# Attention stage of a transformer block: column sums on POOL and VectorE, reciprocals through DRAM, output weights split ahead

## The reference, cut to what matters

```python
q = (xn @ Wq).reshape(B, S, 4, 4, 32); k = (xn @ Wk).reshape(B, S, 4, 32); v = ...
scores = einsum('bqkgd,bskd->bkgqs', q, k) * scale      # causal mask
attn = softmax(scores)                                  # float32
out = einsum('bkgqs,bskd->bqkgd', attn, v).reshape(B, S, 512)
x = x + out @ Wo + moe(xn)
```

## Time and profile before

| what | us |
|---|---|
| median of three runs | 3688.0 |
| the profiled execution | 3685.0 |
| its span, first to last instruction | 3683.2 |
| a full group of stage B (groups 1 to 13) | 128.3 |
| the last group, which has no pieces | 120.0 |
| PE's gap between stages B and C | 22.9 |
| stage C from PE's first matmul | 182.5 |

### The profile page before, as it was taken

The page is one execution under the profiler, slowest core; times in us unless marked ns, Lnnn a source line. Parts: engine busy times, 40 slices in busy tenths (PEclk is TensorE's granted clock), DMA queues, the critical chain, the costliest instruction groups (busy, mean ns, idle before and its releaser), DMA issues. The chain is left out here.

```text
span 3683.2 us, 56527 instructions
## 1 busy us (share of the span) xinstructions
PE 3554.5 (97%) x19856; PEld 2217.2 (60%) x19856; DVE 2357.4 (64%) x5384; ACT 1630.1 (44%) x3341; POOL 2086.6 (57%) x1604
## 2 busy tenths in 40 slices
PE   7999999999997999999999999999999999999699
PEld 5888788888874555555555555555555555554287
DVE  5555554554543455787787778778777877874144
ACT  3222222322321113666665656666565666656511
POOL 0343333332443223877787787778778777878700
PEclk9999999999998999999999999999999999999899
DMA  5333232332329994202211220221122022100176
GB/s 173 100 108 100 100 121 96 110 113 100 108 92 257 293 309 113 50 13 58 53 33 32 56 50 15 56 53 40 25 56 53 16 52 53 41 24 10 56 285 226
DMA packets 228172, 340.55 MB, mean 92 GB/s; under 512 B 65088, under 2 KB 75968, under 8 KB 227968
## 3 DMA queue, kind: packets, MB, share of 16 engines
q1 hardware_dynamic: 197232, 307.77, 27.4%
q0 software_dynamic: 17920, 12.82, 1.7%
q10 hardware_dynamic: 12816, 17.33, 1.3%
HBM read 217.15 MB, written 120.35 MB: 92 GB/s over the span
## 5 line engine op out<-in xcount | busy, mean ns | idle before, releaser
L1350 ACT ACTIVATE prb<-sps 128x512 f32<-128x512 f32 (+3 forms) x2560 | 1187.8, 539 | 753.6 <-PE sps L1448 722.7
L1373 DVE TENSOR_REDUCE mx<-mps 128x1 f32<-128x512 f32 x1440 | 939.9, 681 | 162.0 <-PE mps L1430 162.0
L1294 POOL TENSOR_TENSOR rows<-rows,prb 128x1024 f32<-128x1024 f32 x384 | 908.0, 2386 | 0.0
L388 POOL DMA_INDIRECT tab_s<-pay,slot x384 | 385.6, 1004 | 733.3 <-PE acc L738 419.0
L1376 DVE CUSTOM_DVE_ANT_0 mps<-mps,bias 128x256 f32<-128x256 f32 (+1 forms) x960 | 489.5, 523 | 212.1 <-PE mps L1430 211.9
L1462 PE MATMUL ops<-prb,vst 128*32 128x512 f32 (+3 forms) x5120 | 598.7, 539 | 4.4 <-POOL prb L1279 3.9
L1288 POOL TENSOR_TENSOR rows<-prb 128x1024 f32<-128x1024 f32 x192 | 453.5, 2383 | 149.2 <-ACT prb L1350 149.2
L1430 PE MATMUL mps<-x_lo,w_lo 96*128 96x512 f32 (+2 forms) x1280 | 488.5, 388 | 8.8 <-DVE mx L1373 3.3
L1448 PE MATMUL sps<-w_lo,x_lo 97*128 97x512 f32 (+2 forms) x1280 | 475.3, 392 | 17.6 <-ACT prb L1350 17.6
L1448 PE MATMUL sps<-w_hi,x_hi 97*128 97x512 f32 (+2 forms) x1280 | 482.9, 389 | 9.8 <-ACT prb L1350 8.0
L738 PE MATMUL acc<-x_hi,w_hi 128*128 128x512 f32 x1088 | 431.1, 396 | 9.6 <-DVE qk_lo L584 5.9
(11 more groups left out here) (169 smaller groups left out, 4147.1 us busy)
## 6 DMA issues: line engine op xcount, KB each, us to landing
wgu<-in_e_gu SPq DMA_DIRECT2D x24, 1408.0 KB, 6.9
rows<-in_x SPq DMA_DIRECT2D x16, 1024.0 KB
xn_s<-rows SPq DMA_DIRECT2D x16, 1024.0 KB, 5.1
y_sb<-in_x SPq DMA_DIRECT2D x16, 1024.0 KB
q_hi_s<-qk_hi SPq DMA_DIRECT2D x16, 1024.0 KB
q_lo_s<-qk_lo SPq DMA_DIRECT2D x16, 1024.0 KB
base<-y_sb SPq DMA_DIRECT2D x16, 1024.0 KB, 4.3
w_hi<-q_hi_s SPq DMA_DIRECT2D x64, 256.0 KB
```

Source lines behind the costliest of these rows:

```text
L388: nc.gpsimd.indirect_dma_start(t["tab"], bass.IndirectOffsetOnAxis(ap=slot[:, i, k:k + 1], axis=0), pay[:, i, k, :], None, bounds_check=E ...
L1294: nc.gpsimd.tensor_tensor(acc4, acc4, prb[:, (2 * n + pr) % RP], ALU.add).then_inc(add_done, 1)
L1350: nc.scalar.activation(prb[:, (2 * k + h // 2) % RP, h % 2, q0:CH], sps[:, (GROUP * k + h) % R, q0:CH], ACT.Exp, scale=SCALE).then_inc(exp ...
L1373: V.tensor_reduce(mx[:, h * NKT + qt, j:j + 1], mps[:, n % R, 0:wr], AX.X, ALU.max).then_inc(mred_done, 1)
```

## The change

- **Diagonal tiles.** POOL adds tiles r = 1, 2 and 3 of a block into `dsum` (`add_diagonal`, six adds a block: 768, 512 and 256 columns, for two pairs of heads). PE's new `denominators` sums `dsum` (384 columns a head) and the first 128 columns of tile r = 0, one step after the block's last output. L1467's matmuls are gone.
- **Whole tiles.** POOL does four of the six adds; the last two move to DVE (`add_fourth`, 128x1024 each), at steps f+5 and f+6.
- **Reciprocals.** ACT's copy of `dps` comes one step later, once the sum is done. SP then stores one row for each head (four DMAs of 2 KB), loads them back as 128x16, DVE takes one reciprocal of 128x16 (`invert`, seven steps after the block's last), SP stores that and loads it back spread over the partitions (four DMAs), and POOL multiplies ten steps after the block's last.
- **Order on SP.** `invert` stands ahead of each `store`.
- **Output weights.** w_o and the first attention rows are loaded and split on ACT and DVE in steps 16 to 23 of the last group; the last block's reciprocal and product are done inside stage C.
- `work`, and with it `quota`, is new: steps f+5 and f+6 get fewer pieces, steps 6, 14 and 26 more.

```diff
         work = [1.0 * (CH - max(r, 0) * P) + 1.1 * (CH - max(steps[k - LAG][2], 0) * P) + CH ...][:M1]
-            if any(k - LAG - 1 - part in lasts for part in range(NT)) or LAG <= k < LAG + NT:
-                work[k] -= 400
+            if k - LAG - 1 in lasts or k == LAG:
+                work[k] += 1.1 * CH
+            if k - 5 in fours or k - 6 in fours:
+                work[k] -= 350
 # SP
+            def invert(i, p, j):
+                n = (2 * i + p) * JC + j
+                sp.wait_ge(den_done, n + 2)
+                for h in range(GROUP):
+                    sp.dma_start(t["den"][j % 2, h:h + 1], den[j % 2][HD * h:HD * h + 1, :]).then_inc(den_out, 16)
+                sp.wait_ge(den_out, 16 * GROUP * (n + 1))
+                sp.dma_start(dsm[j % 2][:], t["den"][j % 2].rearrange(...)).then_inc(dsm_in, 16)
+                sp.wait_ge(rsm_done, n + 1)
+                sp.dma_start(t["rec"][j % 2].rearrange(...), rsm[j % 2][:]).then_inc(rec_out, 16)
+                sp.wait_ge(rec_out, 16 * n + 16)
+                for h in range(GROUP):
+                    sp.dma_start(rden[j % 2][HD * h:HD * (h + 1), :],
+                                 t["rec"][j % 2, h:h + 1].to_broadcast([HD, CH])).then_inc(rden_in, 16)
                     for j in range(JC - 1):
+                        invert(i, p, j)
                         store(i, p, j)
...
+                    invert(i, p, JC - 1)
                     store(i, p, JC - 1)
+            sp.wait_ge(s_done, (BG - 1) * NU + 1)
+            for k in range(KC):
+                sp.dma_start(wo[k], t["w_o"][k * P:(k + 1) * P, :]).then_inc(car["wo_in"], 16)
+            sp.dma_start(car["a_in0"].bitcast(F32), t["att"][0, :, :, 0:CH]...).then_inc(car["a_ld0"], 16)
+            for j in range(JC - 1):
+                invert(BG // 2 - 1, 1, j)
+                store(BG // 2 - 1, 1, j)
 # POOL
-                    if k - LAG - NT - 1 in lasts:
-                        normalize(bg, lasts.index(k - LAG - NT - 1))
+                    if k and steps[k - 1][2] > 0:
+                        add_diagonal(bg, k - 1)
+                    if k - SCALED in lasts:                  # SCALED = LAG + 8
+                        normalize(bg, lasts.index(k - SCALED))
+                    if prev and k == SCALED - 1:
+                        normalize(bg - 1, JC - 1)
 # DVE
+            def add_fourth(bg, gi, pr):
+                G, n = bg * NF + gi, fours[gi] + 3
+                dve.wait_ge(add_done, ADDS * G + 3 + pr)
+                dve.wait_ge(exp_done, bg * NU + GROUP * n + 2 * pr + 2 + R)
+                V.tensor_tensor(acc4, acc4, prb[:, (2 * n + pr) % RP], ALU.add).then_inc(fourth_done, 1)
+                    if k - INVERTED in lasts:                # INVERTED = LAG + 5
+                        invert(bg, lasts.index(k - INVERTED))
+                    if prev and k == INVERTED - 1:
+                        invert(bg - 1, JC - 1)
 # PE
+            def denominators(bg, j):
+                pe.wait_ge(dadd_done, 6 * (bg * JC + j + 1))
+                for h in range(GROUP):
+                    M(dps[HD * h:HD * (h + 1), P:CH], ones[:], dsum[:, h // 2, h % 2, P:CH], ...)
+                for h in range(GROUP):
+                    last = M(dps[HD * h:HD * (h + 1), 0:P], ones[:], prb[:, (2 * k + h // 2) % RP, h % 2, 0:P], ...)
```

More of the change, by code:

```diff
@@ L1162, in stage_b @@
         ones = sb("ones_b", [P, HD])
+        wo = att["spare"]
+        EL = GROUP * CH // P
+        dsm = two("dsm", [P, EL])
+        rsm = two("rsm", [P, EL])
+        dsum = sb("dsum", [P, 2, 2, CH])
+        C0 = 16
         sps = ps("sps", [P, R, CH])
@@ L1351, in group @@
                                              sps[:, (GROUP * k + h) % R, q0:CH], ACT.Exp, scale=SCALE).then_inc(exp_done, 1)
-                        for chunk in ended:
-                            if h == 1:
-                                take_denominators(*chunk)
+                        if h == 1 and k - LAG - 2 in lasts:
+                            take_denominators(bg, lasts.index(k - LAG - 2))
+                        if h == 1 and prev and k == LAG + 1:
+                            take_denominators(bg - 1, JC - 1)
                 if not nxt:
@@ new lines, in group @@
+                    todo = list(quota(k)) if nxt else []
+                    for n in todo[:len(todo) // 2]:
+                        reduce(bg + 1, 1 - p, n)
+                    for pr in range(2):
+                        if k - 5 - pr in fours:
+                            add_fourth(bg, fours.index(k - 5 - pr), pr)
+                        for n in todo[len(todo) // 2 + pr:len(todo) // 2 + pr + 1]:
+                            reduce(bg + 1, 1 - p, n)
+                    for n in todo[len(todo) // 2 + 2:]:
+                        reduce(bg + 1, 1 - p, n)
@@ L1464, in output @@
                              skip_group_check=True)
-                if r >= 0:
-                    for h in range(GROUP):
-                        last = M(dps[HD * h:HD * (h + 1), q0:CH], ones[:],
-                                 prb[:, (2 * k + h // 2) % RP, h % 2, q0:CH], start=(r == 0 and j <= 1),
-                                 stop=(r == 3), skip_group_check=True)
                 last.then_inc(pv_done, 1)
@@ L1502, in group @@
                         output(bg - 1, 1 - p, NK + k - LAG)
+                    if k - LAG - 1 in lasts:
+                        denominators(bg, lasts.index(k - LAG - 1))
+                    if prev and k == LAG:
+                        denominators(bg - 1, JC - 1)
                     for n in todo[GROUP:]:
@@ L1512, in group @@
                         output(bg, p, k - LAG)
+                    denominators(bg, JC - 1)
             def ready(bg, p):
@@ L1649, in body @@
                                         ALU.add).then_inc(y_done, 1)
-            low(0, 0)
-            with dve.Fori(0, NC // NQ - 1) as i:
-                body(i, True)
+            body(0, True)
+            dve.wait_ge(den_done, LAST + 2)
+            for part in range(NT):
+                cols = slice(part * P, (part + 1) * P)
+                V.reciprocal(rden[LAST % 2][:, cols], den[LAST % 2][:, cols]).then_inc(rden_done, 1)
+            with dve.Fori(0, NC // NQ - 2) as i:
+                body(i + 1, True)
             body(NC // NQ - 1, False)
```

196 lines of the change are left out of this document (128 added, 68 removed).

## The result

The changed kernel takes 3886.8 us (median of four, 3876.0 to 3894.7) against 3687.9 before (four runs of the same chip): a ratio of 1.0537, 95% interval 1.0518 to 1.0557. It is 199 us slower. I had forecast 3676, and the time lies far outside the range of 3605 to 3722. The profiled execution took 3894.7 us for a span of 3893.0.

The account below looks back on a forecast made before the run. PE, busy 97% of the span, was taken to set groups 0 to 14. Terms -68 + 77 + 0 - 21 = -12 us gave 3673 by the profiled run, 3676 us as median; range 3605 to 3722.

Parts of the forecast that it names:

- Adds on POOL and DVE (even): Full groups: DVE's 12 new adds offset 16 dropped reciprocals, POOL's work stays off the path; 0, between -1 and +3 us a group.
- rival 2: DVE's and POOL's adds exclude each other in full groups; at 2.5 us a group 3713 us, slower; chance 0.22.
- VectorE's own loss: Half a POOL instruction, 1.2 us, lost on each of some six DVE adds: 7 us of DVE a group.
- What PE feels: The part of DVE's lost time that PE's ring of three does not cover, 1.5 to 3.5 us.
- The round trips (+77): Block 0's denominators wait on SP's queue, so DVE then PE stand: 5.5 us a group in groups 1 to 14.
- the walk: Step-by-step timing of block 0's round trip in the eighth group: data land at 2370.2, DVE stands 5.5 us, PE 3.7.
- Column sums (-68): PE's shorter sums of diagonal tiles save 4.5 us a group, ends 3.5 and 5.3, over groups 0 to 14.
- rival 4: PE gains only 3.5 us a group because the exponentials pace the steps; 3691 us, chance 0.10.
- the exponentials' ring: Ring between scores and exponentials: a step that gets shorter than its exponentials gains PE nothing.
- The last group (0): Sums off the ring's path and less POOL backlog offset block 0's late product; 0, between -9 and +6 us.
- The splits on ACT and DVE lie in their idle time: Last group: splitting the early-loaded weights and rows was taken to fit idle time, with no charge.
- Into stage C (-21): PE's 22.9 us gap before stage C shrinks to about 3, half clock partly goes; ends -16 and -23 us.

Follow-up runs that it names:

- before_held: Kernel before the change plus 30 one-operand reciprocals of 128x384 on VectorE, two a group between reductions, no POOL in it; 3760.7 us.
- one_op_block0_late: Changed kernel with VectorE's adds replaced by one-operand reciprocals (output not the reference's) and block 0's reciprocal and product two steps later; 3624.3 us.
- block0_late: Changed kernel with block 0's reciprocal and product two steps later, the other blocks where they were; 3806.0 us.
- prefetch_dram_recip: Kernel before the change with the early loads and splits and the reciprocals through DRAM (block 0's at step 11), column sums as before; 3659.5 us.
- before_prefetch: Kernel before the change with only the early loads and splits, and the last block's reciprocal and product in stage C; 3670.0 us.
- pool_halves: block0_late with each of POOL's adds of 128x1024 made as two of 128x512; 3668.8 us.
- halves_both: pool_halves with each of VectorE's adds also made as two of 128x512, one reduction between them; 3840.6 us.
- one_operand: Changed kernel with each VectorE add replaced by an about equally long one-operand reciprocal of 128x162, output not the reference's; 3716.0 us.
- held_in_halves: Kernel before the change plus 60 one-operand reciprocals of 128x192 on VectorE, four a group, no POOL in it; 3725.3 us.

## Why the prediction was wrong

**The step that failed is "Adds on POOL and DVE (even)"**, 0 with an upper end of +3 us a group, and with it rival 2's price of 2.5. It measured 171 to 182 us, 11 to 12 a group. I had named the mechanism, its place ("the second pair stands just where POOL starts the next run") and its sign in the profile, and gave it 0.22. On the rule itself (the Trainium skill, SBUF — State Buffer, "Who interferes with whom"), the runs agree that the later one waits for the rest of the other, 1.8 us of 2.4, and that one operand does not. The Trainium skill has the first to issue keep the port for its instruction; here an add also waited through several POOL instructions in a row, and the measurement decides. Of the three terms of the price two were too small:

- VectorE's own loss: 7 us forecast, 5.2 measured. That one was about right.
- What PE feels: 1.5 to 3.5 forecast "since DVE has 25 us of slack". before_held shows 0.95 us lost for each us of a 2.5 us hold: PE feels nearly all of a long hold.
- The clock, which I charged behind the round trip but not behind the adds. Against one_op_block0_late a group of after is 17.5 us longer in the mean of groups 0 to 14. Of these 10.0 are PE's busy time (132.9 against 122.9) at a granted clock of 0.93, and only 7.5 idle time. The half clock costs more here than the waits ahead of it.

Why three holds of 2.6 to 3.0 us cost 11 us where two of 2.55 cost 4.8 is not settled. POOL's own adds were delayed too (its busy time in the eighth group was 111.7 us in block0_late, 103.5 in one_op_block0_late); what that cost was not tried.

**The round trips (+77): right.** 81 to 92 us measured; 5.9 us a group (130.8 less 124.9) for 5.5. The walk's issues and landings came 2.0 us apart as forecast. DVE stood 3.6 us instead of 5.5 and PE 2.7 instead of 3.7, while the half clock took 3.4 (126.3 less 122.9 of PE's busy time) instead of 1.3. The data reached DVE 39.4 us after the group's start for 39.5 in the walk, though SP's store was issued 1.1 us later than walked and the four rows took 2.0 us for 3.1, and DVE came to its wait 1.8 us later. The mechanism was right; that the sum came so near is partly luck, since its parts missed in opposite directions.

**Column sums (-68): mis-sized.** A group went from 128.3 to 124.9 us, 3.4 instead of 4.5, so -51: just under my lower end and rival 4's 3.5. Even these 3.4 are not the column sums' alone: the reciprocals through DRAM by themselves took a group from 128.4 to 127.3 us (prefetch_dram_recip), so the sums may be worth as little as 2.3. PE's idle time stayed at 2.0, which speaks against the exponentials' ring; its busy time fell by 3.4 only where I had summed 5.3 from the starts of sets. Where the rest stayed was not tried.

**The last group (0): wrong, +13.** The late product was there (POOL waited 9.3 us for block 0's round trip, and PE at most 3.5 for a select after it). Two things I had not seen. "The splits on ACT and DVE lie in their idle time" left out that a split has two SBUF operands and waits for POOL like an add: in before_prefetch they and the loads made 9 us. And the adds wait there for whole chains; DVE's, POOL's and PE's timeline of after:

```profile
3600.18 16.05 DVE L1476 TENSOR_TENSOR rows<-rows,prb 128x1024 f32<-128x1024 f32 x2 [10.07 <-POOL rows L1358]
...
3605.84 3.63 POOL L1323 TENSOR_TENSOR dsum<-prb 128x768 f32<-128x768 f32 x2
3609.40 0.78 POOL L1336 TENSOR_SCALAR_AFFINE_SELECT prb<-prb 128x256 f32<-128x256 f32 x2
3610.14 3.87 POOL L1323 TENSOR_TENSOR dsum<-dsum,prb 128x512 f32<-128x512 f32 x4
...
3615.23 2.11 PE L1589 MATMUL dps<-rows,ones_b 128*32 128x512 f32 x6 [4.36 <-DVE rows L1476]
```

The first of the two adds took 14.9 us: POOL went from 3597.8 to 3614.0 without a pause, and the add ended 1.1 us later. "DVE rsm <- DMA dsm", 17.5 us in this group, is the longest wait on DVE and costs nothing there, since DVE had no reductions behind it. How the 13 us divide between adds and splits is open: one_op_block0_late, without the adds, still had a last group of 127.4 us.

**Into stage C (-21): right.** The gap is 1.6 us for 22.9, and from PE's first matmul to the end it is 181.8 us for 182.5: -22.

**The sum.** With -51, +85, -22 and +13, and the adds at 0, the time would have been about 3713, inside the range. The adds took it out, and no low chance of a rival can stand in for its price: had I charged rival 2 as I did the round trip, with three waits of 1.8 us felt in full and 0.5 us of half clock behind each, 7 us a group, it would have stood at 3676 + 105 = 3781 and drawn the range with it, still 106 us short of what was measured.

## What to carry to other kernels

Before a two-operand sum or split in SBUF goes to VectorE beside a busy POOL, look at who waits for the instructions behind it: what counts is the rest of POOL's running instruction at that instant, or of its whole unbroken chain, not the mean slack of VectorE. If both must run, cut POOL's instruction and not VectorE's (137 us gained with halves here against 161 lost), and measure it: quarters at some places lost again. And where PE is full on either side, price a wait at more than its length, as a stretch at half clock can follow. In the mean of groups 0 to 14, against before or one_op_block0_late, a group grew by 1.4 times what its idle time grew by in pool_halves (granted clock 1.00), and by 2.1 to 2.5 times in before_held, halves_both, block0_late, after and one_operand (0.93 to 0.99). In held_in_halves it grew by 2.6 us with 0.3 of it idle at a granted clock of 1.00, so not all of PE's added busy time is the clock.

## What the hardware showed that was not expected

- VectorE instructions with two SBUF operands took 14.9 us and 19.8 us, for 1.2 and 0.6 us of work, behind a POOL chain without a pause. Elsewhere (the add of 3.00 us at 2503.29) it got in between two POOL instructions. What decides between the two was not found.
- A PE wait of only 1.75 us in otherwise full work was followed by 3.4 us at a granted clock of 0.53.
- Reciprocals of 128x16 took 0.24 us, twice the eighth of 0.946 that I had put down; it did not matter.
